# Four edits to a one-core graph network kernel: fewer GpSimd pauses, VectorE's sums put ahead of a wait, a row gather and a table load put on other sides of a barrier, group norm statistics in seven parts

## The reference, cut to what matters

```
x = layernorm(x + relu([x, max over edges of (x[dst]-x[src])] @ W0 + b0))            # layer 0
x1 = silu(x @ lin + b); f1, f2 = edge features @ weights
h1 = silu(lin1(sum over edges of f1*x1[src], x1));  h2 likewise with f2
h = cat(h1, h2) @ cat_W + cat_b + x1;  three times: h = silu(h @ lins[i] + b) + h
mean, var of h over all 100,000 nodes, for each of the 128 features                  # group norm
h = norm_w * (h - mean*norm_ms) / sqrt(var + eps) + norm_b
x = layernorm(x + h @ final_W + final_b)                                             # layer 1
x = layernorm(x + relu(sum over edges and self of x@W2 * norm + b2))                 # layer 2
x = layernorm(x + relu(layernorm(sum over edges of x@W3[src]*w + b3)*gamma + beta))  # layer 3
```

## Time and profile before

| | us |
|---|---|
| median of 3 runs (lowest to highest) | 5629.62 (5626.12 to 5631.11) |
| the profiled execution's own time | 5642.86 |
| its span | 5641.1 |
| busy in the span: PE / DVE / ACT / POOL | 4600.9 / 4174.6 / 3699.8 / 4206.8 |
| mean granted TensorE clock (share of 2.4 GHz) | 0.863 |

### The profile page before, as it was taken

One profiled execution on the slowest core, in us unless ns is written; L12 is line 12 of the kernel. 1 busy time (PEld: TensorE's weight loads), 2 busy tenths in 40 slices (PEclk: granted clock), 3 DMA queues, 4 the chain that ended last, 5 costly groups with the idle time before them and its releaser, 6 DMA issues. The chain is left out here.

```text
span 5641.1 us, 87006 instructions
## 1 busy us (share of the span) xinstructions
PE 4600.9 (82%) x20517; PEld 2824.5 (50%) x20517; DVE 4174.6 (74%) x8253; ACT 3699.8 (66%) x9029; POOL 4206.8 (75%) x4707
## 2 busy tenths in 40 slices
PE   7999999999999999999999899999677756662000
PEld 4555555555555544444444377777554544441000
DVE  5666666666666657888888889999788854447776
ACT  4777777777777764444444478888688863336665
POOL 6777777777777757777777467777777767777777
PEclk9999999999999999999999999999855556665555
DMA  4555555555555544655556589999899866665443
GB/s 115 134 136 137 131 131 131 136 137 133 134 127 134 136 125 143 186 180 176 177 179 176 168 324 364 364 367 364 284 287 281 283 209 220 215 221 171 135 135 105
DMA packets 558510, 1084.55 MB, mean 192 GB/s; under 512 B 131182, under 2 KB 225064, under 8 KB 558278
## 3 DMA queue, kind: packets, MB, share of 16 engines
q1 hardware_dynamic: 452918, 931.29, 51.5%
q0 software_dynamic: 100352, 149.23, 11.5%
q10 hardware_dynamic: 5008, 1.60, 0.1%
HBM read 648.47 MB, written 438.76 MB: 193 GB/s over the span
## 5 line engine op out<-in xcount | busy, mean ns | idle before, releaser
L820 ACT ACTIVATE p_s<-p_ps,cols 128x512 f32<-128x512 f32 x588 | 404.0, 687 | 390.3 <-PE p_ps L762 207.8
L682 POOL DMA_INDIRECT home<-edge_row_cols,scatter_cols x392 | 426.0, 1087 | 231.4 <-POOL p_idle L670 155.8
L888 DVE TENSOR_TENSOR p_r<-p_s,p_r 128x512 f32<-128x512 f32 x588 | 402.6, 685 | 220.4 <-ACT p_s L820 199.3
L1155 POOL DMA_INDIRECT ring_rows<-t_rows,home_cols x384 | 450.5, 1173 | 113.8 <-issue 87.8
L175 POOL DMA_INDIRECT u_rows<-t_rows,home_cols x392 | 409.4, 1044 | 146.1 <-issue 117.9
L675 POOL DMA_INDIRECT p_xs<-in_x,src_cols x388 | 412.8, 1064 | 128.9 <-issue 65.7
L175 POOL DMA_INDIRECT ring_rows<-t_rows,home_cols x400 | 396.8, 992 | 146.7 <-issue 115.2
L182 POOL DMA_INDIRECT out<-u_res,scatter_cols x392 | 407.9, 1041 | 121.8 <-issue 118.1
L675 POOL DMA_INDIRECT p_xd<-in_x,dst_cols x388 | 406.8, 1049 | 105.5 <-issue 79.0
L1144 POOL DMA_INDIRECT home_cols<-home,src_cols x380 | 375.1, 987 | 112.8 <-issue 87.6
L1242 ACT ACTIVATE q_s<-q_ps,cols 128x512 f32<-128x512 f32 x294 | 202.0, 687 | 352.6 <-PE q_ps L1219 309.8
(11 more groups left out here) (301 smaller groups left out, 14343.4 us busy)
## 6 DMA issues: line engine op xcount, KB each, us to landing
p_x<-in_x SPq DMA_DIRECT2D x98, 512.0 KB
t_rows<-p_o SPq DMA_DIRECT2D x98, 512.0 KB, 4.5
hT<-p_r SPq DMA_DIRECT2D x98, 512.0 KB
q_hn<-hT SPq DMA_DIRECT2D x98, 512.0 KB
r_h<-hT SPq DMA_DIRECT2D x98, 512.0 KB
r_x<-t_rows SPq DMA_DIRECT2D x98, 512.0 KB
t_rows<-r_y SPq DMA_DIRECT2D x98, 512.0 KB
t_rows<-r_x SPq DMA_DIRECT2D x98, 512.0 KB
```

Source lines behind the costliest of these rows:

```text
L682: nc.gpsimd.indirect_dma_start(out=tab["home"], out_offset=bass.IndirectOffsetOnAxis(ap=s["scat"][:, k:k + 1], axis=0), in_=s["at"][:, k:k ...
L820: nc.scalar.activation(act_out[i][:, :], flat(bank_r), ACT.Silu, bias=col(LS0 + i)).then_inc(r_act[i], 1)
L888: nc.vector.tensor_tensor(hs[i + 1][:, n.of(4 if i == 2 else 2), :], act_out[i][:, :], hs[i][:, n.of(2), :], ALU.add).then_inc(r_added[i], 1)
L1155: nc.gpsimd.indirect_dma_start(out=rows[:, e % 4, j, :], out_offset=None, in_=tab["t1"], in_offset=bass.IndirectOffsetOnAxis(ap=s["home"][ ...
```

## The change

1. nodes01, GpSimd: `pause(j)` pauses only for j = 3. For the gathers that is once behind four transfers, for `map_rows` once behind its second half.
2. nodes01, DVE: L913 and L916 move in front of L906.
3. nodes01, ACT: in the turns behind the last node block the edge block's norm is applied in the even turn instead of the odd one, one turn earlier.
4. The end of nodes01: the `home` table's load goes behind the barrier to the head of edges1's SP program, the wait for the stores of `hT` goes to turn 8 of edges1's SP (and to DVE's first write of the shared tile; the tile of `hs[3]` now lies in `ring_own` slots 4 to 7 in both phases). GpSimd gathers the row numbers of block 3 and the rows of block 1 in front of the barrier too.
5. edges1, GpSimd: in turn t from 4 on first the rows of block t - 2, then the row numbers of block t.
6. edges1: DENSE_LAG is 1: two dense pairs in each of turns 8 to 14, one a turn from 15 to 98. Group norm in seven parts of 42 groups: DVE brings parts 0, 1, 2, 3, 5 together in turns 92 to 96 and part 4 in turn 99, sums six parts there (three small steps), and makes the two factors of `norm_ms` in turn 2. DVE's loop ends at turn 92 instead of 96.
7. edges1 to nodes23: the wait for the stores of `eT` goes behind the barrier, to the head of nodes23's SP. In nodes23 DVE brings only part 6 together (252 elements) and four single-column steps follow instead of six. PE starts the first block's bank with zeros and the eight matmuls as soon as `r_wn` is there, and adds the bias last.

```diff
@@ nodes01, SP @@
-            sp.wait_ge(mapped, DMA * G * EB)
-            home_v = tab["home"].rearrange("(b p h) o -> p b (h o)", p=P, h=2 * G)
-            for c in range(2):
-                sp.dma_start(ring["home"][:, c].rearrange("p (b h) j -> p b (h j)", h=2),
...
                 sp.wait_ge(saved[q], DMA * (NB // 4))
-                sp.wait_ge(h_saved[q], DMA * (NB // 4))
@@ nodes01, GpSimd @@
             def pause(j):
-                if j % 2 == 1:
+                if j == G - 1:
...
             homes(2)
+            homes(3)
             for q in range(2):
                 pool.wait_ge(saved[q], DMA * (NB // 4))
                 pool.wait_ge(e_saved[q], DMA * (EB // 2))
-            pool.wait_ge(to_edges1["homes_in"][0], DMA * G)
-            gather(nc, ring["rows"][:, 0], tab["t1"], s["home"][:, 0:G], to_edges1["rows_in"][0])
+            for b in range(2):
+                pool.wait_ge(to_edges1["homes_in"][b], DMA * G)
+                gather(nc, ring["rows"][:, b], tab["t1"], s["home"][:, b * G:(b + 1) * G], to_edges1["rows_in"][b])
@@ nodes01, ScalarE @@
-                if not even and e.live(EB):
+                if even == (t.fixed and t.b >= NB) and e.live(EB):
@@ nodes01, VectorE, in front of L906 @@
+                n, q = t, t.pair()
+                if n.live(NB):
+                    c = n.slot % 2 * G
+                    dve.wait_ge(product, n.b + 1)
+                    after(dve, applied, n.b - 3)
+                    nc.vector.tensor_tensor(v[:, n.of(4)], bank_o[:, :, :], to4(s["b0"]), ALU.add).then_inc(biased, 1)
+                    dve.wait_ge(biased, n.b + 1)
+                    dve.wait_ge(x_in[q.of(2)], landed(2, q))
+                    nc.vector.scalar_tensor_tensor(v[:, n.of(4)], v[:, n.of(4)], 0.0, x[:, n.of(4)],
+                                                   ALU.max, ALU.add).then_inc(summed, 1)
@@ edges1 @@
-        MASK_AT, DENSE_AT, DENSE_LAG = 5, 8, 3
-        STEPS = EB + DENSE_LAG
+        MASK_AT, DENSE_AT, DENSE_LAG = 5, 8, 1
+        STEPS = EB + 3
@@ edges1, SP @@
+            home_v = tab["home"].rearrange("(b p h) o -> p b (h o)", p=P, h=2 * G)
+            for c in range(NC):
+                sp.dma_start(home[:, c].rearrange("p (b h) j -> p b (h j)", h=2),
+                             home_v[:, c * NB // 4:(c + 1) * NB // 4, :]).then_inc(home_in[c], DMA)
             for t in range(EB + 10):
+                if t == DENSE_AT:
+                    for q in range(2):
+                        sp.wait_ge(hT_saved[q], DMA * (NB // 4))
...
-            for q in range(4):
-                sp.wait_ge(h_saved[q], DMA * len(range(q, EB, 4)))
@@ edges1, VectorE @@
+            PART = (NB + EB) // PARTS
+            SUM_FROM = LOOP_TO - UNROLL
+            PART_AT = {SUM_FROM: 0, SUM_FROM + 1: 1, SUM_FROM + 2: 2, SUM_FROM + 3: 3, SUM_FROM + 4: 5, EB + 1: 4}
+
+            def gather_part(i):
+                end = (i + 1) * PART
+                if i * PART < NB:
+                    dve.wait_ge(n_counted, min(end, NB))
+                after(dve, e_counted, end - NB)
+                part_of_stats(nc, s, i).then_inc(gathered, 1)
...
                 for m in pairs[:1]:
                     mask_pair(m)
+                if t.fixed and t.b in PART_AT:
+                    gather_part(PART_AT[t.b])
@@ nodes23, PE @@
+                if i == 0:
+                    pe.wait_ge(cleared, 2)
+                    nc.tensor.matmul(bank, s["ones3"][:, :], zeros3[:, :], start=True, stop=False)
+                    pe.wait_ge(weights, 1)
+                else:
+                    nc.tensor.matmul(bank, s["ones3"][:, :], bias, start=True, stop=False)
                 for j in range(G):
                     i_mm = nc.tensor.matmul(bank_n[i % 2][:, j, :], h[:, i % 6, tile(j)], wn[:, :],
-                                            start=False, stop=j == G - 1)
+                                            start=False, stop=i > 0 and j == G - 1)
+                if i == 0:
+                    pe.wait_ge(weights, 2)
+                    i_mm = nc.tensor.matmul(bank, s["ones3"][:, :], bias, start=False, stop=True)
@@ nodes23, VectorE @@
-            then(nc.vector.bn_aggr(small[:, MEAN:VAR + 1], s["stats"][:, :, :].rearrange("p b c -> p (b c)")))
-            then(nc.vector.scalar_tensor_tensor(c1(M2), c1(MEAN), c1(MEAN), c1(VAR), ALU.mult, ALU.add))
...
+            then(part_of_stats(nc, s, PARTS - 1))
+            then(nc.vector.scalar_tensor_tensor(squares, means, means, squares, ALU.mult, ALU.add))
+            then(nc.vector.tensor_tensor(small[:, MEAN:M2 + 1], s["sums"][:, :], s["parts"][:, PARTS - 1, :], ALU.add))
+            then(nc.vector.scalar_tensor_tensor(c1(K2), c1(MEAN), s["shares"][:, 1:2], c1(MEAN), ALU.mult, ALU.mult))
+            then(nc.vector.scalar_tensor_tensor(c1(V2), c1(M2), SHARE, c1(K2), ALU.mult, ALU.add))
```

111 lines of the change are left out of this document (64 added, 47 removed).

## The result

The changed kernel takes 5538.49 us (median of 4 runs, 5533.12 to 5540.03) where the kernel before took 5628.72 (median of 4, 5626.12 to 5631.11): a ratio of 0.984, 95% interval 0.982 to 0.986, so 90 us. In a later sitting it took 5535.86 against 5631.06, ratio 0.983 (0.9815 to 0.9845). Forecast was 5547. The profiled execution of the changed kernel took 5533.12 us.

The account below looks back on a forecast made before the run. GpSimd was taken to pace nodes01, with TensorE next; transfers bound nodes23. 61 + 13.5 - 3.0 - 0.5 + 11.8 = 82.8 us off 5642.86, with the median 13.2 lower, gave 5547 us (5530 to 5562; 8 in 10 reaching 5588).

Parts of the forecast that it names:

- GpSimd is the pacer, TensorE is next: Nodes01: GpSimd's loop of 20.68 us a pair sets the pace; TensorE's 20.05 is the floor, gaining 61 us.
- The pauses: Nodes01, GpSimd: three of six pauses a pair go, 0.3 us a pair, 29 us over 97 pairs.
- Rival 1: GpSimd stays nodes01's pacer with as much held time; only the pauses' 29 us come there, 5579 in all; chance 0.27.
- The held time: Nodes01: GpSimd instructions beginning inside VectorE ones with two SBUF inputs wait, some 1.5 us a pair; 1.15 may stay.
- my sign for it: Nodes01: the power L707 would stand idle with VectorE as its releaser, at a pair near 20.05 us.
- The order: Nodes01: L913 and L916 leave the piece between power and residual 1, so TensorE bears a power 1.4 us later.
- Rival 2: Nodes01: by the skill page's lock rule L916 waits for the power; GpSimd stays the pacer, 5579; chance 0.04.
- The border to edges1: Nodes01 to edges1: earlier start 4.5 us plus turn 2's stall and cold clock 9.0, 13.5 us (8 to 14).
- The table behind the barrier: End of nodes01: moving the `home` table's load frees SP sooner, TensorE starts near 2096.5, gain 4.5 us.
- The dense turns: Edges1: turns with two dense pairs cost 1.5 us each too much; seven instead of five, -3.0 us.
- The parts of the norm: Edges1, turns 92 to 96: some 1.2 us each against VectorE's 1.0 us to spare, -0.5 us (0 to -2).
- The border to nodes23: Edges1 to nodes23: last dense pair 2.4, smaller norm step 7.3, bias behind matmuls 2.1; 11.8 us, 8 at the low end.

Follow-up runs that it names:

- e2: The changed kernel with L913 and L916 back behind the step that waits for the power, fewer pauses kept: 5542.84 us, ratio 0.985 to the kernel before.
- e4: The changed kernel with no pause at all in nodes01: 5529.54 us, ratio 0.983 to the kernel before.
- e9: The kernel before with L916 reading TensorE's product in PSUM instead of L913's sum in SBUF: 5630.74 us, ratio 1.000.
- e8: The changed kernel with the bias of nodes23's first block in front of its eight matmuls again: 5530.54 us, ratio 0.983 to the kernel before.
- e5: The changed kernel with the wait for the squares' stores moved from the end of nodes01 to the loads in edges1: 5530.66 us, ratio 0.982.

## Why the prediction was right, and where its steps were not

- **GpSimd is the pacer, TensorE is next.** Right. In before GpSimd waits for no one; in after, e2 and e4, with different loads on GpSimd, the pair is 19.91 to 19.93: TensorE's pace. I had 20.05. The mis-sized piece is the 17.45 us taken from L742 at 1504.57 as if nothing in it were late: that L742 took 1.13 us and the half pair to the next L742 is 10.53 us in the earlier trace rows, in after 10.43 (1509.47 to 1519.90). The pair won 0.73 us (20.64 to 19.91) where I had 0.63. With 64 us in the 88 steady pairs and 9 in the first ten, nodes01 gave 73.5 where I had 61; the 75 of my upper end held it.
- **The pauses.** I put 0.3 us a pair on them. The distances give 0.38, since the pause in front of the `xs` gathers cost 0.21 and not 0.09; the term was low by a fifth. Rival 1, the kernel with the pauses' 29 us and nothing more, fell because the held time fell with them.
- **The held time.** It had to fall by 0.35 of 1.5 us. The 1.5 was too much: it counts 16 transfers a pair where there are twelve, over a free length of 0.94 where transfers that begin in no VectorE instruction take 0.99. By 12 x 0.994 = 11.93 the transfers were held for 0.93 us in before, and the power for 0.12. The twelve fell by 0.79 (12.86 to 12.07), so nearly all of it went, where I had found "about 1.1 us held" by laying one pair out. GpSimd went past TensorE's pace and had to wait. The prediction named no reason why the time should fall this far: that it did was in its favour, and not foreseen. It waits in front of the gathers of `xs`, not of the power; my sign for it was in the wrong place, because I had not asked which of GpSimd's waits comes first once it runs ahead.
- **The order.** The prediction gave it a role (a power may come later by 1.4 us) that it does not play: in the steady pairs of after VectorE never waits for the power (L928 has no idle time from 300 to 1950 us), since GpSimd is ahead. With the pauses there it gives 42 us by shorter GpSimd instructions and distances, with the fewer pauses 7.0, all but 0.6 of it in the first ten pairs.
- **The rule against the change.** The Trainium skill (SBUF — State Buffer, "SBUF: two separate sides") lets whichever of VectorE and GpSimd comes second wait for the first. e9 agrees for GpSimd as the second (1.274 us down to 0.971 when one VectorE input leaves SBUF). For VectorE as the second the rows here do not agree: 0.69 us inside a power, 40 times in before and 120 times in after. L920, the old L916, takes 0.69 us on average and never more than 0.72. Rival 2 did not come.
- **The border to edges1.** 13.5 us forecast, 11.1 measured (84.6 - 73.5). The stall of turn 2 and the cold clock gave 9.3 (I had 9.0). The table behind the barrier gave 1.8 where I had 4.5. The step that failed is "both row gathers run from 2083.4 to 2093.4, before VectorE ends": the transfers do end 0.9 us before VectorE, but GpSimd's drain ends 4.6 us behind them. I took the end of the last transfer for the end of the engine. The ScalarE edit was not undone by itself in any run, so what it gives is not shown.
- **Edges1.** The dense turns cost 4.7, not 3.0, in this trace; in seven others of the same turns 2.1 to 6.5, so 3.0 lies inside the scatter and the 4.7 corrects nothing. What was wrong is the even 1.5 us a turn: it mixes turns that cost 1 us with turns in which `ends` is late and that cost 1.5 to 4.5. The parts of the norm cost nothing: turn 92 and turn 97 have the same difference, -81.0.
- **The border to nodes23.** 11.8 forecast, 11.6 measured (91.6 - 80.0 by TensorE's end of edges1, 9.3 by VectorE's, which itself ends earlier by the 2.3 of the dense pair), with 2.07 for the bias by e8.
- **Later phases.** Nodes23 gave back 3.1 us in this profile, 1.8 in the second profile of the changed kernel (90.4 at the first `r_v`, 88.6 at the last) and 3.0 in e5 against after; with e4 it gave back 0.7. From its first to its last `r_v` nodes23 takes 772.3 to 778.5 us in the ten traces of the changed kernel and its variants, and 772.5 and 772.9 in before and e9. Most of the 3.1 is scatter, but a loss of 2 to 3 us by the change, for which I have no cause, is not excluded.

The sum by the marks is 73.5 + 11.1 - 4.7 + 1.1 + 10.6 - 3.1 - 1.2 = 87.3 us. The forecast's 82.8 misses it by 4.5, from larger errors of both signs: 12.5 too little in nodes01, 2.4 too much at the first border, 1.7 at the dense turns, 4.3 lost behind edges1, and 0.4 net on the other two terms (the parts of the norm and the border to nodes23). The mechanism of nodes01 (GpSimd the pacer, TensorE's pace the floor) was right; that the total is as close as it is, with nodes01 12.5 us off, is luck.

## What to carry to other kernels

An engine that paces a loop by waiting for nobody can be slowed by where its instructions fall against another engine's, and taking one such collision away may only move it to the next; what paid here was to get the engine ahead until it had a wait of its own. Before work is moved in front of a barrier, look at the drain of the engine that gets it, and not at the end of its last transfer. Extra work that catches up on a schedule is best spread to the amount that the slack of one turn holds: three blocks were free, four cost 1.4 to 2.0 us a turn. Look also at which load stands behind the extra loads in the queue, since up to half of that cost lay in turns where one load came late.

## What the runs showed that I had not expected

- GpSimd's drain behind indirect DMAs: it ends 3.2 to 4.6 us behind the last transfer, and where it is the last drain TensorE's first instruction of the next phase follows 1.09 us behind it.
- A transfer that begins inside a VectorE instruction with two SBUF inputs takes longer by what is left of that instruction less some 0.14 us (1.27 us with 0.43 left, 0.99 with none running); with one input in PSUM, or inside a scan, 0.95 to 1.01.
- One chip ran the kernel before at 6101 us (11 runs, 6090 to 6142) and two edited versions at 6266 (one of its six runs at 19487) and 6407: there they are slower than before, by 2.5% and 5.1%. In nodes01 TensorE is busy for 450 of 500 us in the version that joins the edits, where it is busy for 499 on the other chip:

```profile
1500.00:2000.00 500.00, 450.37 (x1889) 260.43 (x1888) 289.84 (x512) 324.92 (x623) 309.06 (x278) 0.98 0.46 119
```

```profile
DVE p_ve L955 <- remote: 40.1, 12, 5.0
ACT p_s L831 <- remote: 39.6, 15, 5.1
```

VectorE and ScalarE wait there up to 5 us at a time (us in total, times, longest) for something that the trace cannot name, and no row of this kind stands in the same window of the same kernel on the other chip. Nodes23, where the transfers set the pace, is no longer there: 777.3 and 776.1 us from its first to its last `r_v`. Neither the cause nor why the edited versions should lose there is settled; the changed kernel itself did not run on that chip.
